# Attention with adaptive layer norm: block 6 of the second query half moved from the GpSimd adds into TensorE's sums product

## The reference

```python
att = jnp.einsum('bhgqd,bhkd->bhgqk', qg, k) / math.sqrt(D_HEAD)
att = jnp.where(causal[None, None, None], att, -jnp.inf)
probs = jax.nn.softmax(att, axis=-1).astype(resid.dtype)
ctx = jnp.einsum('bhgqk,bhkd->bhgqd', probs, v)
```

## Time and profile before

| what | value |
|---|---|
| three runs | 2493.58, 2493.68, 2498.49 us |
| median | 2493.68 us |
| the profiled execution's own time | 2495.66 us |
| its span in the trace | 2493.9 us |
| mean granted TensorE clock | 0.99 |
| busy: TensorE, VectorE, ScalarE, GpSimd | 2406.7, 1723.4, 1042.6, 1650.8 us |

### The profile page before, as it was taken

One profiled execution on the slowest core, in us unless ns is written; L12 is line 12 of the kernel. 1 busy time (PEld: TensorE's weight loads), 2 busy tenths in 40 slices (PEclk: granted clock), 3 DMA queues, 4 the chain that ended last, 5 costly groups with the idle time before them and its releaser, 6 DMA issues. The chain is left out here.

```text
span 2493.9 us, 36376 instructions
## 1 busy us (share of the span) xinstructions
PE 2406.7 (97%) x13140; PEld 1668.3 (67%) x13204; DVE 1723.4 (69%) x3392; ACT 1042.6 (42%) x1873; POOL 1650.8 (66%) x865
## 2 busy tenths in 40 slices
PE   5999999999999999999999999998999999999998
PEld 3788888887555555555555555544788788888886
DVE  4866666677888888888888888874555355455553
ACT  3433333231666666666666666665211111111111
POOL 3744333441799998999989999993655455545643
PEclk8999999999999999999999999999999999999999
DMA  6532333352545325344233345313333333323330
GB/s 236 198 118 87 115 113 118 123 150 80 162 100 146 82 64 154 83 132 97 71 79 83 83 117 132 84 31 127 112 92 101 103 90 97 118 86 104 107 93 25
DMA packets 179727, 267.45 MB, mean 107 GB/s; under 512 B 20508, under 2 KB 113884, under 8 KB 178400
## 3 DMA queue, kind: packets, MB, share of 16 engines
q1 hardware_dynamic: 179552, 265.13, 36.2%
HBM read 183.22 MB, written 80.81 MB: 106 GB/s over the span
## 5 line engine op out<-in xcount | busy, mean ns | idle before, releaser
L1082 POOL TENSOR_TENSOR p_sum<-p_sum,p_ring 128x1024 f32<-128x1024 f32 (+2 forms) x465 | 991.3, 2164 | 71.0 <-PE ctx_ps L1143 50.2
L976 ACT ACTIVATE p_ring<-scores 128x512 f32<-128x512 f32 (+1 forms) x896 | 448.9, 568 | 236.3 <-DVE scores L1030 173.6
L272 DVE TENSOR_REDUCE neg_max<-scores_q 128x1 f32<-128x512 f32 x679 | 438.8, 684 | 79.0 <-PE scores_q L253 64.9
L253 PE MATMUL scores_q<-k_stack,q_stack 96*128 96x512 f32 (+1 forms) x1473 | 443.0, 378 | 14.6 <-DVE neg_max L269 6.3
L1122 PE MATMUL scores<-q_stack,k_stack 98*128 98x512 f32 (+1 forms) x1216 | 409.7, 414 | 10.6 <-ACT p_ring L976 7.7
L253 PEld LDWEIGHTS scores_q<-k_stack,q_stack 96*128 96x128 f32 x1473 | 263.6, 191 | 135.4 <-DVE neg_max L269 64.5
L1122 PEld LDWEIGHTS scores<-q_stack,k_stack 98*128 98x128 f32 x1216 | 205.9, 190 | 184.7 <-ACT p_ring L976 71.9
L627 POOL TENSOR_TENSOR roped_hilo<-roped_hilo 128x512 fp32r<-128x512 f32 x80 | 105.5, 1319 | 337.0 <-ACT roped_hilo L467 337.0
L269 DVE CUSTOM_DVE_ANT_0 scores_q<-scores_q,masks 128x512 f32<-128x512 f32 x489 | 296.0, 642 | 38.4 <-PE scores_q L253 38.4
L676 PE MATMUL proj_ps<-h_hi,w_hi 128*128 128x512 f32 x752 | 298.7, 397 | 0.7 <-POOL w_lo L616 0.7
L676 PE MATMUL proj_ps<-h_hi,w_lo 128*128 128x512 f32 x752 | 294.1, 391 | 0.0
(11 more groups left out here) (182 smaller groups left out, 3632.8 us busy)
## 6 DMA issues: line engine op xcount, KB each, us to landing
q_stack<-qk_t SPq DMA_DIRECT2D x96, 512.0 KB, 6.8
qk_t<-roped_hilo SPq DMA_DIRECT2D x80, 512.0 KB, 2.8
x_in<-in_L_attn_resid SPq DMA_DIRECT2D x32, 512.0 KB, 6.3
ctx_t<-ctx_raw SPq DMA_DIRECT2D x64, 256.0 KB, 5.4
prefetched<-in_L_wmod SPq DMA_DIRECT2D x4, 4096.0 KB, 13.6
prefetched<-ctx_t SPq DMA_DIRECT2D x31, 512.0 KB, 4.0
prefetched<-inv_t SPq DMA_DIRECT2D x124, 128.0 KB, 5.5
k_stack<-qk_t SPq DMA_DIRECT2D x96, 128.0 KB, 8.8
```

The lines of the kernel that those rows point to most:

```text
L253: last = nc.tensor.matmul(dst[:, a, :], qs[0:MHI, h, i * P:(i + 1) * P], ks[0:MHI, lo:lo + w], start=not first and (a == 0 or not diag), s ...
L272: nc.vector.tensor_reduce(neg, src, AX.X, ALU.max, negate=True).then_inc(sh.s_mx.sem, 1)
L976: nc.scalar.activation(p[:, a * per:(a + 1) * per, :], src[:, a * per:(a + 1) * per, :], ACT.Exp, scale=SM_SCALE).then_inc(s_ex.sem, 1)
L1082: nc.gpsimd.tensor_tensor(a, a, probs(n, u), ALU.add).then_inc(s_ap.sem, 1)
```

## The change

The tail of the second half begins at key block 6 instead of 7.

```diff
-TAIL_FROM = {0: 4, 1: 7}
+TAIL_FROM = {0: 4, 1: 6}
```

## The result

The changed kernel takes 2505.12 us (median of six executions, 2502.11 to 2509.83) against 2493.63 us of the kernel before (six, 2492.46 to 2499.21). The measured ratio is 1.0037, with an interval of 1.0022 to 1.0051 (the quotient of the two medians alone is 1.0046; both lie in the interval). The forecast was 2504.7 us. The profiled execution of the changed kernel is the slowest of its six: 2509.83 us, with a span of 2508.0.

The account below looks back on a forecast made before the run. TensorE's in-order queue was taken to bound the attention stage at the sums product. Added products of 13.3 us less 2.3 at the end gave +11.0 us, a forecast median of 2504.7 us (+0.44%), range 2500.0 to 2508.5.

Parts of the forecast that it names:

- TensorE sets the period at this place: At the second half's sums product, all three other engines wait for TensorE's in-order queue; period 33.50 us.
- 0.43 us per block, 31 times: Added 256-column products for four heads on TensorE in groups 0 to 30: 13.3 us, all on the path.
- the upper bound with a change of kind (0.79): Most the added block could cost, in us, if it also paid the tail's change to the next kind of product.
- Removed adds worth nothing in an ordinary group: 31 GpSimd adds of 2.383 us go, 73.9 us of busy time, with no gain on the path in ordinary groups.
- GpSimd's wait near 3.9 us: GpSimd's wait per period for TensorE's first values product was to grow from 1.03 to about 3.9 us.
- shifted, not shortened: VectorE's 1.28 us and ScalarE's 0.88 us waits at the sums product were to keep their lengths and come later.
- The gain at the end, 2.27 us: In group 31, TensorE's 2.45 us wait for GpSimd before group 30's sums product goes, save a 0.18 us gap.
- what is late next?: Step for group 31's end: remaining adds finish at 1691.03, TensorE is ready at 1691.90, so the wait goes.
- The sum: Whole kernel: 13.3 us for the products less 2.3 at the end, +11.0 us.
- Hidden product: Rival: the 0.43 us block disappears in TensorE's pauses and only the end's gain stays, 2491.4 us; chance 0.08.
- VectorE relieved: Rival: GpSimd's adds hold a port VectorE needs, so removing them gives up to 73.9 us, 2430.8 us; chance 0.02.
- Dearer product: Rival: block costs 0.6 to 0.79 us, 2513.1 us, or TensorE's clock falls once more, 2506.4 us; chance 0.10.

Follow-up runs that it names:

- at unit 13: Sums product moved from unit 9 to 13 of the following group: kernel before 2502.54 us (ratio 1.0022), changed kernel 2514.11 us (1.0073).
- the second profiles: Both kernels executed and profiled again, nothing changed: kernel before 2497.45 us (one execution), changed kernel 2504.77 us, ratio 1.0046.
- two settings by group: Against the kernel before: no tail in groups 0 to 22, then from block 7, 2491.22 us; the same with block 6 too in groups 29 and 30, 2492.06 us.
- the product too: Against the kernel before: GpSimd's add of block 6 kept and its product on TensorE made as well; 2506.56 us, ratio 1.0045.

## Why the prediction was right, and where it was not

- **TensorE sets the period at this place.** Right, and shown: the product costs the same with the add kept (33.95) and the period is unchanged with only the add gone (33.53).
- **0.43 us per block, 31 times.** Right: 33.96 - 33.50 = 0.46 in the first pair of profiles, 33.95 - 33.54 = 0.41 in the second, 12.4 us over 29 periods where 12.5 were due, 0.43 again at unit 13, and 0.64 for 384 columns. The row of the same shape in the last group gave the price; the upper bound with a change of kind (0.79) didn't come true.
- **Removed adds worth nothing in an ordinary group.** Right. 72.9 us of GpSimd's adds went (991.3 to 918.4), and its idle time grew. The detail "GpSimd's wait near 3.9 us" holds as a sum in two places: 3.18 + 0.80, because GpSimd now also catches up with ScalarE's exponentials before the adds of the next group's first half.
- **VectorE's and ScalarE's waits "shifted, not shortened".** Half right. They were not shortened, but they didn't stay at 1.28 and 0.88 either; they grew to 1.71 and 1.31. Both engines have finished their own work by the time the added block starts (ScalarE at 1165.46, VectorE at 1165.89, the block at 1165.86), so it lengthens their wait by its whole 0.43. The prediction moved the waiting engines along with the product, though they aren't behind it.
- **The gain at the end, 2.27 us.** This term was mis-sized. The wait did go. But from the last but one tail product to the end of the attention only about 1.0 us was won: 54.59 us on the mean of the two profiles of before, plus 0.86 for two blocks, against 54.49. The two profiles of before are 1.5 us apart in this stretch, so this is no sharper than 1 us or so. In the run with only the add gone the same stretch gave 1.8 us. The step that failed is "what is late next?". It took TensorE's arrival, 1691.90, as fixed, and all that follows the product as fixed too. The arrival already held 1.7 us of low clock, and in the changed kernel a longer wait for the transfer came in front of it (1.99 us instead of 1.10), with 8 us at 0.53 behind that. And the 23.67 us behind the product are the short case: the second profiles have 25.22 and 25.67 (0.43 of the latter for the added block), with another fall of the clock. Both vary from one execution to the next, and before the change the wait for GpSimd hid the first of them.
- **The sum.** The stage grew by 12.3 us, 31 blocks of 0.43 less the 1.0. Between the medians there are 2505.12 - 2493.63 = 11.5 us, against +11.0. By the ratios it is 9.2 us (5.5 to 12.7) in the first measurement and 11.5 (7.0 to 16.0) in the second. So the main term is confirmed by the periods; that the median of the sum came out within 0.5 us is partly luck, because the term of the end was 1.3 us too large, which the medians' own scatter covers.
- **The rivals.** Hidden product: no, at no place that was tried. VectorE relieved: no. Dearer product: no for the block. Its other branch, one more fall of the clock, did occur in the first profile of the changed kernel (8 x (1 - 0.53) = 3.8 us of lost clock in its worst stretch). It isn't why this execution is the slowest of six: of the 5.4 us that its span is above that of the second profile, 4.8 lie in the first stage and 0.7 in the attention.

## What to carry to other kernels

When two engines both look full, see which of them waits at the place of the change: work moved from the one that waits to the one that is waited for costs its full length, here 0.43 us times 31 for 73 us of freed GpSimd time that nothing could use. A single wait at the end of a loop can be worth less than its length, because it also covers whatever else was late there: here 2.45 to 3.96 us of wait went, and about 1.0 us was won. An engine that is slower per round than the one it feeds doesn't hold it up at once, as long as it has a lead and longer groups refill it; look at how the lead develops and not at one round. And where the balance between two engines differs along a loop, set it group by group: none of the three other settings for all groups (from block 6, from block 5, no tail) beat the kernel before, and two settings by group did.

## What I had not expected

- TensorE's granted clock falls from 1.00 to 0.50 behind the thin stretch around the transfer wait ahead of group 31, for a length that isn't fixed. The same kernel averaged 0.53 over 8 us in one execution and 0.86 in the other; the last period was 30.66 us in the first and 28.53 in the second.
- The transfer into `q_stack` ahead of group 31 made TensorE wait 1.10 us in the kernel before and 1.99 and 2.28 us in the changed one (2.57 with the product too). It doesn't go with the tail's length alone: with block 5 as well the wait is 1.12 us again. Why it is later there stays open.
- The kernel with a change in one group of the attention (block 6 of group 30) has its own stage as it was, and a stage behind it that is 4 to 9 us longer, twice, with pauses of 3 to 4 us between matmuls that wait for nothing which the profile shows. Spans of single kernels that differ by 0.2% can come from such places, so the stages have to be compared one by one.
